# Stack stages: probabilities divided before their transposes, value products that give the context transposed, inverse roots from logarithm, exponential and a Newton step

## The reference, cut to what matters

```python
q, k, v = split(shift_tokens(x) @ Wqkv[i])        # 16 heads of 64
q, k = l2norm(q) * q_scale[i], l2norm(k) * k_scale[i]   # then rotary with a scale
# l2norm(t) = t / max(norm(t), 1e-12)
sim = 8.0 * q_block @ k_window.T                  # local windows, masked
attn = softmax(sim)
out = attn @ v_window
x = out @ Wo[i] + x
x = (a * gelu(gate)) @ W2[i] + b2 + x             # with a layer norm and W1 ahead
```

## Time and profile before

| what | value |
|---|---|
| median of 3 runs | 5570.57 us (5566.59 to 5572.81) |
| the profiled execution | 5569.76 us |
| its span, first to last instruction | 5568.0 us |
| mean granted PE clock | 0.957 of full speed |
| 43 steps of the first stack stage, 1187.11 to 2775.55 us | 1588.44 us |
| 43 steps of the second, 3271.53 to 4859.75 us | 1588.22 us |

### The profile page before, as it was taken

The page is one execution under the profiler, slowest core; times in us unless marked ns, Lnnn a source line. Parts: engine busy times, 40 slices in busy tenths (PEclk is TensorE's granted clock), DMA queues, the critical chain, the costliest instruction groups (busy, mean ns, idle before and its releaser), DMA issues. The chain is left out here.

```text
span 5568.0 us, 144442 instructions
## 1 busy us (share of the span) xinstructions
PE 5171.8 (93%) x50580; PEld 3628.8 (65%) x50580; DVE 3788.9 (68%) x7798; ACT 3321.5 (60%) x5490; POOL 3101.5 (56%) x1917
## 2 busy tenths in 40 slices
PE   8988968599999999999978699999999999989889
PEld 5655645277777777777755377777777777756556
DVE  3343336588888888888855588888888888855545
ACT  3343323377777777777745377777777777742542
POOL 0000015488888888888830488888888888820200
PEclk9989977699999999999989899999999999989899
DMA  1000000111111111111100111111111111110000
GB/s 42 4 1 32 1 7 2 39 43 53 45 48 50 53 45 52 46 46 55 39 20 1 39 43 53 45 53 45 53 49 49 45 50 54 37 39 1 7 24 8
DMA packets 110452, 197.67 MB, mean 36 GB/s; under 512 B 21408, under 2 KB 28848, under 8 KB 110256
## 3 DMA queue, kind: packets, MB, share of 16 engines
q1 hardware_dynamic: 110256, 194.99, 12.3%
HBM read 53.29 MB, written 1.05 MB: 10 GB/s over the span
## 5 line engine op out<-in xcount | busy, mean ns | idle before, releaser
L2678 POOL TENSOR_TENSOR stage_qk<-stage_halves 128x1024 f32<-128x1024 f32 x384 | 905.5, 2358 | 489.7 <-DVE stage_halves L2760 489.7
L2689 POOL TENSOR_TENSOR stage_rnorm<-stage_clamped,minus_half 128x16 f32<-128x16 f32 x384 | 1116.1, 2907 | 32.0
L2696 POOL TENSOR_TENSOR stage_qk<-stage_qk,stage_rnorm 128x1024 f32<-128x1024 f32 x384 | 730.1, 1901 | 22.5
L2554 ACT ACTIVATE stage_probsT<-stage_flip 96x512 f32<-96x512 f32 x768 | 453.4, 590 | 296.8 <-PE stage_flip L2312 296.8
L2516 ACT ACTIVATE stage_square<-stage_wide 128x1024 f32<-128x1024 f32 x384 | 392.8, 1023 | 363.6 <-PE stage_wide L2260 355.4
L2757 DVE TENSOR_TENSOR stage_halves<-stage_wide,stage_tables 128x1024 f32<-128x1024 f32 x384 | 468.1, 1219 | 106.4 <-ACT stage_square L2516 66.9
L2326 PE MATMUL stage_pv<-stage_v_win,stage_probsT 96*64 96x65 f32 x12288 | 527.1, 228 | 4.8 <-DVE stage_context L2791 4.6
L2326 PEld LDWEIGHTS stage_pv<-stage_v_win,stage_probsT 96*64 96x64 f32 x12288 | 420.5, 137 | 138.8 <-issue 133.0
L2277 PE MATMUL stage_turn<-ident,stage_qk 128*128 128x128 f32 x3072 | 483.8, 280 | 27.9 <-ACT stage_qkT L2536 6.7
L2760 DVE TENSOR_TENSOR stage_halves<-stage_wide,stage_tables 128x512 f32<-128x512 f32 x768 | 490.5, 680 | 0.0
L2277 PEld LDWEIGHTS stage_turn<-ident,stage_qk 128*128 128x128 f32 x3072 | 351.0, 141 | 195.5 <-issue 83.7
(11 more groups left out here) (296 smaller groups left out, 9589.4 us busy)
## 6 DMA issues: line engine op xcount, KB each, us to landing
stage_v_win<-stage_v SPq DMA_DIRECT2D x384, 195.0 KB, 2.6
stage_v_win<-stage_v SPq DMA_DIRECT2D x384, 130.0 KB, 2.4
stage_v_win<-stage_v SPq DMA_DIRECT2D x192, 65.0 KB, 2.2
stage_wq<-in_T_wq SPq DMA_DIRECT2D x12, 512.0 KB, 4.1
stage_wk<-in_T_wk SPq DMA_DIRECT2D x12, 512.0 KB, 3.4
stage_wv<-in_T_wv SPq DMA_DIRECT2D x12, 512.0 KB, 3.5
stage_wo<-in_T_wo SPq DMA_DIRECT2D x12, 512.0 KB, 3.4
stage_w_up<-in_L_w_up SPq DMA_DIRECT2D x8, 512.0 KB, 7.2
```

What stands on the lines that cost most here:

```text
L2554: nc.scalar.activation(probsT[:, n % 2].rearrange("p h t q -> p (h t) q"), tiles4(flip)[0:REACH], ACT.Copy)\
L2678: nc.gpsimd.tensor_tensor(qk[:, n, :], halves[:, n % 2, 0, :], halves[:, n % 2, 1, :], ALU.add)\
L2689: nc.gpsimd.tensor_tensor(rnorm[:, n, :], clamped[:, n, :], chip.minus_half[:, :].to_broadcast([P, LH]), ALU.pow)\
L2696: nc.gpsimd.tensor_tensor(heads, heads, rnorm[:, n, :].rearrange("p (h o) -> p h o", o=1).to_broadcast([P, LH, LD]), ALU.mult).then_inc(at ...
```

## The change

Three parts of stage_stack change, and the order of each engine's loop is written anew.

First, the probabilities are divided before they are transposed. DVE sums them for each row and takes the reciprocal (sum_probs, four times a step, on 128x768 values), POOL multiplies (normal_probs), and turn_probs waits for POOL's signal "normal" instead of ACT's "probs". The column of ones in v and v_win goes, with one memset.

Second, the value product is turned round: v_win is the stationary operand and probsT the moving one, so the result is the context transposed. divide, turn_context and the tile context go, and copy_ctxT reads the bank pv. The products of two pairs of heads lie in one bank, and weigh waits for ctxT at every second pair.

Third, the inverse root: POOL clamps as before (clamp); ACT takes Ln and then Exp with scale -0.5 (first_root, four times a step on 128x16 values); POOL improves it by a Newton step of four operations (refine) in place of the ALU.pow operation. deviation, the inverse root of the layer norm, keeps ALU.pow.

Besides, lay_band writes both banks with one ACT instruction in place of two.

```diff
-        v, v_win = sb("v", [P, HALVES, LH, LD + 1]), sb("v_win", [REACH, BLOCKS, LH, LD + 1])
+        v, v_win = sb("v", [P, HALVES, LH, LD]), sb("v_win", [REACH, BLOCKS, LH, LD])
...
-        pv = pv_psum[:, 0:4 * (LD + 1)].rearrange("p (h t c) -> p h t c", h=2, t=HALVES)
+        pv = pv_psum[:, :].rearrange("p (n s) -> p n s", n=2)
...
             def turn_probs(step, n):
-                pe.wait_ge(*att("probs", step, n // 2 + 1))
+                pe.wait_ge(*att("normal", step, n // 2 + 1))
...
             def weigh(step, n):
...
-                pe.wait_ge(*att("context", step, n))
-                for h in range(2):
-                    for t in range(HALVES):
-                        for c in range(2):
-                            block = slice(c * QBLOCK, (c + 1) * QBLOCK)
-                            ins = nc.tensor.matmul(pv[block, h, t, :], probsT[:, n % 2, h, t, block],
-                                                   v_win[:, 2 * t + c, 2 * n + h, :], start=True, stop=True,
-                                                   skip_group_check=True)
+                if n % 2 == 0:
+                    pe.wait_ge(*att("ctxT", step, n // 2))
+                for block in range(BLOCKS):
+                    t, of_block = block // 2, slice(block % 2 * QBLOCK, (block % 2 + 1) * QBLOCK)
+                    for h in range(2):
+                        ins = nc.tensor.matmul(pv[h * LD:(h + 1) * LD, n % 2, block * QBLOCK:(block + 1) * QBLOCK],
+                                               v_win[:, block, 2 * n + h, :], probsT[:, n % 2, h, t, of_block], start=True, stop=True,
+                                               skip_group_check=True)
...
+            def first_root(step, n):
+                act.wait_ge(*att("clamped", step, n + 1))
...
+                nc.scalar.activation(logs[:, n, :], clamped[:, n, :], ACT.Ln).then_inc(att["logs"], 1)
+                act.wait_ge(*att("logs", step, n + 1))
+                nc.scalar.activation(root[:, n, :], logs[:, n, :], ACT.Exp, scale=-0.5).then_inc(att["root"], 1)
...
             def lay_band(step, m):
                 act.wait_ge(*att("shifted", step, m))
-                for h in range(2):
-                    ins = nc.scalar.activation(score_psum[:, h, 0:2 * HALVES * REACH], band[:, :, :].rearrange("p t k -> p (t k)"), ACT.Copy)
-                ins.then_inc(att["banded"], 1)
+                both = band[:, :, :].rearrange("p (o t) k -> p o t k", o=1).to_broadcast([P, 2, 2 * HALVES, REACH])
+                nc.scalar.activation(scores, both, ACT.Copy).then_inc(att["banded"], 1)
...
-                act.wait_ge(*att("ctxT_psum", step, j + 1))
-                nc.scalar.activation(ctxT[:, 2 * j:2 * j + 2, :], turn[:, :].rearrange("p (c s) -> p c s", c=2), ACT.Copy)\
+                act.wait_ge(*att("pv", step, 2 * j + 2))
+                nc.scalar.activation(ctxT[:, 2 * j:2 * j + 2, :], pv, ACT.Copy)\
...
-                nc.gpsimd.tensor_tensor(rnorm[:, n, :], clamped[:, n, :], chip.minus_half[:, :].to_broadcast([P, LH]), ALU.pow)\
-                  .then_inc(att["rnorm"], 1)
+            def refine(step, n):
+                y, to = root[:, n, :], refined[:, n, :]
+                pool.wait_ge(*att("root", step, n + 1))
...
+                nc.gpsimd.tensor_tensor(to, clamped[:, n, :], y, ALU.mult).then_inc(att["by_root"], 1)
+                pool.wait_ge(*att("by_root", step, n + 1))
+                nc.gpsimd.tensor_tensor(to, to, y, ALU.mult).then_inc(att["squared"], 1)
+                pool.wait_ge(*att("squared", step, n + 1))
+                att.settle(pool)
+                nc.gpsimd.tensor_scalar(to, to, -0.5, 1.5, ALU.mult, ALU.add).then_inc(att["correction"], 1)
+                pool.wait_ge(*att("correction", step, n + 1))
+                nc.gpsimd.tensor_tensor(rnorm[:, n, :], to, y, ALU.mult).then_inc(att["rnorm"], 1)
+            def normal_probs(step, m):
+                pool.wait_ge(*att("rsum", step, m + 1))
+                nc.gpsimd.tensor_tensor(probs[:, m % 2], probs[:, m % 2], rsum[:, m % 2].to_broadcast([P, 2, 2 * HALVES, REACH]), ALU.mult)\
+                  .then_inc(att["normal"], 1)
...
-            def divide(step, n):
...
+            def sum_probs(step, m):
+                dve.wait_ge(*att("probs", step, m + 1))
...
+                nc.vector.tensor_reduce(sums[:, m % 2, :, :, 0], probs[:, m % 2], AX.X, ALU.add).then_inc(att["sums"], 1)
+                dve.wait_ge(*att("sums", step, m + 1))
+                nc.vector.reciprocal(rsum[:, m % 2], sums[:, m % 2]).then_inc(att["rsum"], 1)
```

More of the change, by code:

```diff
@@ L2445, in body @@
                 if runs(s):
-                    turn_probs(s, 6)
-                if runs(e):
-                    up(e, 0)
+                    turn_probs(s, 5)
+                if runs(s):
+                    weigh(s, 4)
                 if runs(u):
@@ L2451, in body @@
                     turn_qk(u, 5)
+                if runs(e):
+                    up(e, 2)
                 if runs(s):
-                    turn_probs(s, 7)
-                if runs(s):
-                    weigh(s, 6)
+                    turn_probs(s, 6)
                 if runs(u):
@@ L2617, in body @@
                 if runs(s):
-                    copy_probsT(s, 5)
-                if runs(s):
-                    exponential(s, 3)
+                    copy_probsT(s, 4)
                 if runs(u):
@@ L2623, in body @@
                 if runs(w):
-                    squares(w, 0)
+                    squares(w, 1)
+                if runs(e):
+                    gate(e, 1)
                 if runs(u):
@@ L2633, in body @@
                 if runs(e):
[L2634 removed]
+                    gate(e, 2)
                 if runs(s):
[L2636 removed]
+                    copy_probsT(s, 6)
                 if runs(w):
[L2638 to L2652 removed]
+                    first_root(w, 0)
                 if runs(w):
@@ L2655, in body @@
                 if runs(u):
+                    copy_qkT(u, 6)
+                if runs(u):
+                    lay_band(u, 1)
+                if runs(s):
+                    copy_ctxT(s, 2)
+                if runs(s):
+                    copy_probsT(s, 7)
+                if runs(u):
+                    exponential(u, 0)
+                if runs(w):
+                    first_root(w, 1)
+                if runs(u):
+                    copy_qkT(u, 7)
+                if runs(s):
+                    copy_ctxT(s, 3)
+                if runs(w):
+                    squares(w, 3)
+                if runs(u):
+                    lay_band(u, 2)
+                if runs(u):
+                    exponential(u, 1)
+                if runs(w):
+                    copy_qkT(w, 0)
+                if runs(u):
                     copy_probsT(u, 0)
+                if runs(w):
+                    first_root(w, 2)
             for s in range(-2, 2):
```

321 lines of the change are left out of this document (142 added, 179 removed).

## The result

The changed kernel takes 5918.07 us (median of 4 runs, 5911.17 to 5932.37) against 5569.49 us for the kernel before (4 runs): a ratio of 1.0631, 95% interval 1.0616 to 1.0646. It is 349 us slower where 236 were forecast. The profiled execution took 5932.37 us, with a span of 5930.6.

The account below looks back on a forecast made before the run. PE bounded the kernel before; ACT would bound the changed one: 28.7 us of work plus 10.0 of loads, then 0.7 of waits, 39.4 a step, 2.46 more, times 96, 236 us: 5806 us, range 5620 to 6110.

Parts of the forecast that it names:

- The mechanism: Ln and Exp on ACT reload tables at each change, 9 loads a step in place of 2, making the kernel slower.
- rival A: One table serves Ln and Exp, loads stay two a step, PE stays the bound: 35.3 us a step, 5412 us; chance 0.15.
- ACT becomes the bound: With seven further table loads ACT needs 38.7 us a step, more than PE's 34.99, and sets the pace.
- PE, 34.99 us: PE's work in a step: 36.94 less 1.95 for the dropped context transposes, with weigh taken as unchanged.
- 0.3 us of new waits for PE: If loads stay two a step, PE might wait 0.3 us a step behind normal_probs, making 35.3.
- POOL, 28.9,: POOL's work in a step: 30.04 less 11.63 for powers, plus 4.8 for refine and 5.7 for normal_probs.
- DVE, 30,: DVE's work in a step stays at 30 us: 4.8 us of divisions go, 4.6 of sums and reciprocals come.
- Loads, 7 x 1.43 = 10.0 us: Seven further table loads a step on ACT at changes between Ln and Exp, 1.43 us each, 10.0 us.
- Waits left, 0.7 us: ACT's remaining waits in a step, 0.7 us, as most of its 9.9 us of waits vanish under the loads.
- the sum 39.4: The forecast step of the changed loop: 39.4 us, 2.46 more than before.
- rival B: PE, waiting in order, also drops to clock 0.84: 42.5 us a step, 6104 us; chance 0.12.
- a busy share of 89%: PE busy 35 of 39.4 us, as in an earlier stretch at granted clock 0.84, taken as the case for a lower clock.

Follow-up runs that it names:

- one_table: The changed kernel with one table named for Ln and Exp, 2 loads a step in place of 9; 5365.75 us, ratio 0.9624 to the kernel before.
- filled: The changed kernel with the first query and key projection of each step issued twice, as extra PE work; 5844.11 us, ratio 1.0490 to the kernel before.
- idle_loads: As one_table, with two further loads a step of the same table where ACT idles, 4 in all; 5365.31 us, ratio 0.9625 to the kernel before.
- stop_at_3: As one_table, but part 3's inverse root alone switches tables twice, ahead of copy_probsT, 4 loads a step; 5662.65 us, ratio 1.0160 to the kernel before.
- pow_again: The changed kernel with the third part undone, ALU.pow back on POOL, no Ln, 2 loads a step; 5628.22 us, ratio 1.0097 to the kernel before.
- part3_alone: The kernel before with only the third part (clamp, first_root, refine), one table named, 2 loads a step; 5621.62 us, ratio 1.0089 to the kernel before.

## Where the prediction was right, and where not

**The mechanism** was right in kind, and the runs show it: the loads come at Ln and Exp, nine a step; PE is no longer the bound; with the seven loads alone taken away +6.3% turns into -3.8%. one_table makes rival A true by hand; A's forecast was 5412 us, 35.3 us a step, and it came out at 5365.75. "ACT becomes the bound" was half of it: of the 39.38 - 34.44 = 4.94 us that the stops add to a step, ACT's busy time above PE's step is 36.91 - 34.44 = 2.47, and in the other half ACT and PE wait for each other.

**PE, 34.99 us.** In one_table, where PE is always busy, the step is 34.44, so PE saved 2.50 us and not 1.95. turn_context was right (its slots add up to 1.99 a step in the trace of before). The missed term is weigh, taken as unchanged with a bound of 0.08: from start to start it takes 4.66 us a step in one_table and took 5.29. A pair of heads alone still takes 0.61 to 0.62. In the new order four of the eight follow each other in twos (32 matmuls in 1.08 to 1.12 us), which none did before; that is some 0.3 us. And two of the eight took 0.76 and 0.84 before, which is the rest. I costed the instruction and left out its neighbours. This, and 0.3 us of new waits for PE that did not come, is more than the 46 us by which A's own forecast was too slow.

**POOL, 28.9,** measured 27.6: refine's small operations take 0.20 to 0.22 us, and the 0.08 that the prediction added to each for the wait before it is idle time, not busy time. **DVE, 30,** measured 30.8. normal_probs was put at 1.43 and took 1.469. A root without loads was put at 0.5 and takes 0.4.

**Loads, 7 x 1.43 = 10.0 us.** Measured as busy time 8.76, 1.25 each. ACT without the loads, 28.7, was 28.15. So ACT is busy 36.91 in the changed kernel (36.75 in filled), where the prediction had 38.7.

**Waits left, 0.7 us.** This step failed. A step without low clock takes 39.38, so ACT stands idle for some 2.5 us of it. The prediction took ACT as nearly packed; it is not, since PE's delays at the three places come back to it (64.9 us of waits for the flips in 43 steps). ACT's sum is a floor and not the law: idle_loads and stop_at_3 have the same number of loads and almost the same ACT sum (1317 and 1326 us) and differ by 297 us. That the sum 39.4 met the undisturbed step of 39.38 is luck, two errors that cancel: 1.8 us too much busy time, 1.8 too little idle.

**The clock, rival B.** It was given 0.12 as another case, with the whole step at 0.84. It came in small, inside the forecast: 0.97 and 0.96 on the mean, as 3.35 us at 0.50 behind one wait. The steps put it at 0.87 and 1.33 us; over 96 steps that is some 106 us, about the 112 us by which the result lies over 5806. The pattern looked for, a busy share of 89%, was the wrong one: the changed kernel has PE busy 90% at 0.97, not at 0.84; filled has it busy 94% at 1.00, and stop_at_3, at 94% as well, has low clock in about every second step. What differs is the longest single wait of PE. In filled it is 0.9 us, in pow_again 1.1 to 1.3, and neither has a low clock in its loops; every low stretch in the loops of the other runs stands behind a wait of 1.8 to 2.2 us. Rival B's PE at a low clock for the whole step did not come.

**By steps,** 96 x (39.38 - 36.94) = 234 us for the stops, against 236 forecast, and the rest is the clock and the 0.2 us by which the second half's steps are longer.

**The price of a switch.** A load takes 1283 ns in the traces of before and after (x384 at Ln's and at Exp's line after). From the load's start to the logarithm's are 4024.18 to 4025.47, 1.29 us. Left to itself the changed kernel loads at each Ln and at each Exp behind it, 344 times in its first 43 steps; in one_table, with the table named, there is no load at either line.

**Open.** Why the second half's steps take 0.2 us more (34.65 against 34.44 in one_table; from start to start it lies in one flip, 0.64 in place of 0.55, and in the product with wo, 3.55 in place of 3.47); what each of the first two parts is worth by itself, which wasn't tried; whether part3_alone loses nothing with its other roots moved; and why the same wait is followed by low clock in some steps and not in others.

## What to carry to other kernels

Count the table loads before you move a function to ACT, and name one table for the functions that alternate; here one line, put into the loop and once ahead of it, was worth 552 us. Then look at what stands right behind a load in ACT's order and who waits for it: two loads in idle time cost nothing (idle_loads), and two ahead of a copy that PE needs cost 3 us a step with ACT busy for 82% of it (stop_at_3). And when an engine is given short gaps, look at the granted clock behind each gap, not at its mean over the stage.

## What the hardware showed beyond this

- A load of the table that is already loaded takes its 1.28 us all the same (idle_loads, 198 loads at the two added lines, 1283 ns each).
- In the changed kernel PE standing still for 2.21 us in a stretch of 4.06 was followed by 3.35 us at half clock; with the gap filled by repeated work (wait 0.49 us) the clock stayed at 1.00 and the kernel was 1.3% faster for doing more (5918.07 to 5844.11).
- The same wait of 2.2 us is followed by low clock in about every second step of stop_at_3, in 28 of 43 steps of the changed kernel's first half and in all 43 of its second; what else decides isn't settled.
- Waits of PE of 0.9 us (filled) and 1.1 to 1.3 us (pow_again) in every step left the clock at 1.00.
